# Moving the four combined quarters of x of each batch from VectorE to GpSimd

## The reference

```
h       = gelu(x @ fc1_w.T + fc1_b)                    # 512 -> 2048
x       = x + concat(h @ fc2_w.T + fc2_b,              # 384 shared columns
                     h @ experts_w[idx].T + experts_b) # 128 columns of the batch's expert
scores  = tanh(x @ W1 + b1) @ v
p       = softmax(scores under the mask of the batch: l <= j, l >= j or l != j)
x       = x + (p @ x) / count(mask)
```

## Time and profile before

| | us |
|---|---|
| median of 3 runs | 1362.59 (1361.64 to 1362.98) |
| the profiled execution's own time | 1362.06 |
| its span, first to last instruction | 1360.3 |
| PE busy | 1348.4 (99%) |
| DVE busy | 1231.0 (90%) |
| ACT busy | 868.7 (64%) |
| POOL busy | 0.2 (0%) |

### The profile page before, as it was taken

How to read it: one execution, slowest core, us unless ns; L and a number is a source line. 1 busy time by engine, 2 the same in 40 slices (tenths; PEclk the granted TensorE clock), 3 DMA queues, 4 the chain that set the end, 5 groups by cost and what they waited for, 6 DMA issues and landing times.

```text
span 1360.3 us, 22015 instructions
## 1 busy us (share of the span) xinstructions
PE 1348.4 (99%) x8734; PEld 869.8 (64%) x8734; DVE 1231.0 (90%) x2057; ACT 868.7 (64%) x1493; POOL 0.2 (0%) x4
## 2 busy tenths in 40 slices
PE   9999999999999999999999999999999999999998
PEld 4348476584766748567584765848567584765856
DVE  7896889899898998989899898998989999898998
ACT  4867848477583756838477483766838468483753
POOL 0000000000000000000000000000000000000000
PEclk9999999999999999999999999999999999999999
DMA  8410011110201102011020201102011020200001
GB/s 292 149 37 33 1 63 32 39 56 1 78 17 55 40 1 78 16 63 32 19 76 1 71 25 47 48 0 78 17 62 32 9 78 9 66 29 14 25 10 55
DMA packets 29192, 62.98 MB, mean 46 GB/s; under 512 B 5922, under 2 KB 6690, under 8 KB 26658
## 3 DMA queue, kind: packets, MB, share of 16 engines
q1 hardware_dynamic: 28658, 61.05, 13.8%
q10 hardware_dynamic: 432, 0.53, 0.1%
HBM read 44.79 MB, written 16.78 MB: 45 GB/s over the span
## 4 chain that ended last, share of the span: by engine, by line
PE 90%; DVE 7%; ACT 2%; DMA 1%; issue 0%; ACTq 0%; DVEq 0%
PE ps L394 14%; PE ps L396 14%; PE ps L395 14%; PE ps L313 13%; PE ps L314 13%; PE ps L315 13%; PE ps L284 1%; PE ps L431 1%; PE ps L426 1%; PE ps L596 1%; PE ps L422 1%; PE ps L421 1%; PE ps L420 1%; DVE hl L1062 1%; DMA er<-in_w 1%; DVE mx L1001 0%
## 5 line engine op out<-in xcount | busy, mean ns | idle before, releaser
L394 PE MATMUL ps<-hh,w2l 128*128 128x512 f16 x768 | 291.3, 379 | 0.7 <-ACT ps L623 0.7
L396 PE MATMUL ps<-hl,w2h 128*128 128x512 f16 x768 | 291.2, 379 | 0.0
L395 PE MATMUL ps<-hh,w2h 128*128 128x512 f16 x768 | 291.2, 379 | 0.0
L313 PE MATMUL ps<-xh,w1h 128*128 128x256 f16 x960 | 261.8, 273 | 0.0
L314 PE MATMUL ps<-xl,w1h 128*128 128x256 f16 x960 | 261.8, 273 | 0.0
L315 PE MATMUL ps<-xh,w1l 128*128 128x256 f16 x960 | 261.8, 273 | 0.0
L647 ACT ACTIVATE g<-ps,b1s,ds 128x512 f32<-128x512 f32 x240 | 173.5, 773 | 99.5 <-PE ps L315 98.5
L313 PE MATMUL ps<-xh,ch 128*128 128x256 f16 x720 | 196.4, 273 | 0.6 <-ACT ps L623 0.3
L315 PE MATMUL ps<-xh,cl 128*128 128x256 f16 x720 | 196.3, 273 | 0.0
L314 PE MATMUL ps<-xl,ch 128*128 128x256 f16 x720 | 196.3, 273 | 0.0
L1062 DVE SCALAR_TENSOR_TENSOR hl<-g,ix,hh 128x512 f16<-128x512 f32 x244 | 177.3, 739 | 1.6
(11 more groups left out here) (208 smaller groups left out, 2343.3 us busy)
## 6 DMA issues: line engine op xcount, KB each, us to landing
xr<-in_xT SPq DMA_DIRECT2D x62, 256.0 KB, 3.1
er<-in_ew SPq DMA_DIRECT2D x15, 1024.0 KB, 5.6
out<-xr SPq DMA_DIRECT2D x60, 256.0 KB, 2.4
raw<-in_w SPq DMA_DIRECT2D x28, 256.0 KB, 6.2
er<-in_w SPq DMA_DIRECT2D x3, 1024.0 KB, 10.1
xr<-in_ew SPq DMA_DIRECT2D x1, 1024.0 KB, 5.7
out<-er SPq DMA_DIRECT2D x3, 256.0 KB, 2.5
xr<-in_xT ACTq DMA_DIRECT2D x2, 256.0 KB, 5.1
```

What stands on the lines that cost most here:

```text
L313: mm(to, wh, mh, start=i in (1, 5) and c == 0, stop=False, skip_group_check=True)
L394: mm(po(b, o), wl, hh[:, k, :], start=False, stop=False, skip_group_check=True)
L395: mm(po(b, o), wh, hh[:, k, :], start=False, stop=False, skip_group_check=True)
L396: m = mm(po(b, o), wh, hl[:, k, :], start=False, stop=k == NH - 1, skip_group_check=True)
```

## The change

`combine` leaves VectorE's program. A new program on GpSimd runs the four subtractions of each batch 1 to 15, with the same operands and buffers. It waits for the loads of x, for the last low part of h of the batch before (`hl_done`), and where one combination reads another, for that one. For batch 1 it waits for the first four tiles of h of batch 0, those whose buffers are used. What waits for the combinations on ScalarE and VectorE is unchanged.

```diff
-        def combine(b, t):
-            for c in range(KD):
-                e.wait_ge(x_in[b % XB * KD + c], x_loaded(b))
-            if b > 1:
-                e.wait_ge(hl_done, nth_tile(b - 1, NH - 1))
...
-            tt(combined(t), x, y, ALU.subtract).then_inc(combos)
...
         batch_scales(1)
-        combine(1, T1)
-        combine(1, T2)
         expert_low(0, 1)
         pads()
         masks()
-        combine(1, T3)
-        combine(1, T4)
         expert_low(0, 2)
...
             batch_scales(b + 1)
-            for t in (T1, T2, T3, T4):
-                combine(b + 1, t)
             pool(3)
...
+    def gpsimd_program(eng):
+        e = Engine(eng)
+
+        def combine(b, t):
+            for c in range(KD):
+                e.wait_ge(x_in[b % XB * KD + c], x_loaded(b))
+            e.wait_ge(hl_done, nth_tile(b - 1, NH - 1) if b > 1 else nth_tile(0, GR - 1))
+            if t == T1:
+                x, y = quarter(b, 0, 1), quarter(b, 0, 0)
+            elif t == T2:
+                e.wait_ge(combos, 4 * (b - 1) + 1)
+                x, y = quarter(b, 1, 1), combined(T1)
+            elif t == T3:
+                x, y = quarter(b, 1, 1), quarter(b, 0, 1)
+            else:
+                e.wait_ge(combos, 4 * (b - 1) + 2)
+                x, y = quarter(b, 1, 0), combined(T2)
+            eng.tensor_tensor(combined(t), x, y, ALU.subtract).then_inc(combos)
+
+        for b in range(1, B):
+            for t in (T1, T2, T3, T4):
+                combine(b, t)
```

More of the change, by code:

```diff
@@ L1620, in _ @@
             vector_program(eng)
+        @block.gpsimd
+        def _(eng):
+            gpsimd_program(eng)
 def kernel(x, itok_B_0_15, itok_B_0_2, L0_cond_fc1_w, L0_cond_fc1_b, L0_cond_fc2_w, L0_cond_fc2_b,
```

## The result

| | before | after |
|---|---|---|
| median, us | 1362.3 | 1407.68 (1407.05 to 1410.08, 4 runs) |
| ratio | | 1.0338, interval 1.0325 to 1.0351 |
| span of the profiled execution, us | 1360.3 | 1405.3 |
| PE busy, us | 1348.4 | 1362.5 |

A forecast was written before the change was run, and what follows sets the result against it. TensorE, never idle, was taken as the bound, VectorE's saving as worth 0. Waits of 46.8 us (batches 2 to 14), 4.0 (batch 1) and 2.5 (opening), together 53.3, on 1362.06 gave 1415 us, range 1372 to 1430.

The forecast's parts named there:

- TensorE is the bound, a saving on VectorE buys nothing, a wait adds in full: Whole kernel: TensorE has no idle time, so VectorE's freed 2.4 us per batch gain 0 and each new wait lengthens the run.
- GpSimd's duration, 1.22 us: One moved subtraction on GpSimd takes 1.22 us, as VectorE's scan; four take 4.9 us and finish before their readers.
- The delay d, 4.88 us: Pooling steps and bounds after the last low part of h: GpSimd's reading makes VectorE's bounds end 4.88 us later.
- I take the whole: Between bounds of 0 and 4.9 us, VectorE's delay was taken as all of GpSimd's work, four operations alternating with six.
- The room of 1.28 us: Before the sum of line 278, batches 2 to 14: VectorE's bounds may be 1.28 us late before TensorE waits.
- Batch 1, 4.0 us: At batch 1's sum: the delay of 4.88 us less a room of 0.89 costs 4.0 us.
- The opening, 2.5 us: Opening, at low parts of w1: about half of GpSimd's 4.9 us delays TensorE, 2.5 us, between 0 and 4.9.
- TensorE's busy time unchanged at 1348: Profile after: the loss shows as TensorE idle time before line 278, while its busy time stays at 1348 us.
- No collision that matters: Rival at the bounds: both engines read beside each other, delay under 1.28 us, not slower, 1362 us; chance 0.16.
- Sharing: Rival at the bounds: both engines run at about two thirds speed while both read, delay 2.4 us, 1379 us; chance 0.19.
- The dear case: Rival at the bounds: a GpSimd operation takes nearer 2 us and excludes VectorE, delay 7 us, 1446 us; chance 0.06.
- Faster: Rival: VectorE's freed 2.4 us per batch help, at most some 1 us in the opening, 1361 us; chance 0.02.

The follow-up runs named there:

- the control: Kernel before, VectorE still making the combinations, plus four idle two-input subtractions on GpSimd in batches 2 to 15: 1409.56 us, ratio 1.0349.
- the copy: Kernel before, VectorE still making the combinations, plus four one-input copies of quarters of x on GpSimd in batches 2 to 15: 1362.14 us, ratio 1.0004.
- the memset: Kernel before, VectorE still making the combinations, plus four memsets without inputs on GpSimd in batches 2 to 15: 1362.30 us, ratio 1.0001.

## Why the prediction was right, and where its terms were not

- **TensorE is the bound, a saving on VectorE buys nothing, a wait adds in full.** Shown for batches 2 to 14: the three kernels with extra work on VectorE stall by d - 1.28 in each, and the control with the combinations on VectorE as well has the changed kernel's distances. In the opening a wait doesn't add in full, since TensorE has other waits there that get shorter.
- **GpSimd's duration, 1.22 us.** Right: 1.23 from start to start when undisturbed, 1.27 by its record. It was in part luck, since the value was VectorE's scan's and no row of GpSimd; the 1.1 us estimated beside it is too low. The combinations were never late; no wait of ScalarE for them is in the trace.
- **The delay d, 4.88 us.** Mis-sized: 3.75. "I take the whole" was the step that failed. A GpSimd subtraction holds one step of VectorE by 0.89 to 1.01 us here, not by its whole 1.22; why the rest of it is no loss, no view shows. The mechanism, one GpSimd operation in between two of VectorE, is what the timeline shows; the copy and the memset show that for steps with two inputs it is the reading.
- **The room of 1.28 us.** Right, to 0.02: with d of 1.90, 1.93 and 3.75 the batches grow by 0.63, 0.65 and 2.47. 13 stalls are 32.0 us, not 46.8.
- **Batch 1, 4.0 us.** It was 1.37. There d is 9.15 - 6.34 = 2.81. All four hold VectorE there, by 1.02 to 1.07 us each and 4.2 together, but before the change VectorE stood idle for 1.26 us ahead of the bounds, which takes up a part (the row below). The prediction took d in batch 1 to be that of the others and missed this wait. Of 2.81 go 0.89 of room, and the 0.54 that is taken up behind the opening.

```profile
153.05 0.17 DVE L1046 TENSOR_SCALAR sq<-sq 128x8 int32<-128x8 int32 x1 [1.26 <-ACT xl L691]
```

- **The opening, 2.5 us.** It was 1.56 by the sum, and by other parts. Two of the four operations hold VectorE, as forecast, for 2.07 us together, which is what the wait for w1 grows by; half clock behind it adds 1.7, and the shorter waits of the opening take up the rest.
- **TensorE's busy time unchanged at 1348.** Wrong, and the term that wasn't in the sum: half the clock behind every second stall, 9.9 us of the 14.1 by which the busy time grew. Another 1.7 is the half clock of the opening, and the rest is mostly stall that modelled ends of matmuls count as busy (2.47 - 2.29, 13 times). The kernel with six extra operations shows that the stall alone brings the half clock. It made up for half of the 18 us by which the other terms were too large. So that 1415 came within 8 us of 1407.7 is luck in part: two errors had opposite signs. Without the clock behind the 13 stalls, and with the measured d, batch 1 and opening, the same working gives 1397.
- **The rivals.** "No collision that matters" is refuted for subtractions; for memsets and copies it holds in the time, though not in VectorE's durations. "Sharing" had d at 2.4 and no alternation; the measured d lies between it and exclusion. "The dear case" had GpSimd at nearly 2 us, against 1.27. "Faster" had nothing to stand on.

## What to carry to other kernels

On a kernel whose TensorE is never idle, first find the wait that ends last in the stretch into which moved work falls, and its room (here 1.28 us); an operation on a second engine costs by what it takes from the first, not by its own time. Work with SBUF inputs on GpSimd isn't off VectorE: here four subtractions saved VectorE 2.4 us and took 3.75, at the worst place. And a stall of TensorE of some 2 us should be priced with a loss of clock behind it: here 0.8 us on average for a stall of 2.47, and 2.4 for one of 4.26.

## What the runs showed of the hardware

- GpSimd's 128x512 f32 operations: a subtraction 1.27 us undisturbed, 1.31 to 1.72 beside VectorE's two-input operations, 2.19 beside its scans; a copy 0.67 at least, 1.07 beside such steps; a memset 0.53.
- What GpSimd's subtractions hold on VectorE: scalar_tensor_tensor and tensor_tensor with two inputs (0.69 to 0.75 us become 1.64; 128x128, 0.29 becomes 1.35), the tensor_scalar with one tensor input (0.48 to 1.49), scans (1.22 to 2.04), and tensor_scalar operations on eight and four elements (0.16 to 1.27 and 1.11). The hold of some 1 us hardly depends on the size of VectorE's operation. Not held: tensor_reduce of 128x512, 0.67 before GpSimd starts and beside it. Beside memsets, only the tensor_scalar was seen to be held (1.81 us, in 2 of 13 batches).
- The granted clock of TensorE at 0.50 behind stalls of 2.3 us, every second time and for 3.4 us, and of 4.1 us, every time and for some 5; never behind 0.5 us. Behind the wait of 1.8 us that all 14 kernels have near their end (line 596 before) it was at 0.50 in two. What decides at 2.3 us is left open; the turns were strict in all three kernels with batches 84.5 and 86.2 us apart.
